# One VectorE subtraction of 1024 columns written as two of 512, in a fused gate-and-FFN kernel on one Trainium2 core

## The reference

```python
ctx   = causal_ema(x, tau_ctx)                        # h[t] = alpha*h[t-1] + x[t]
gated = x * sigmoid(concat([x, ctx]) @ Wg.T + bg)
h1    = gelu(x @ Wn1.T + bn1)
mod   = 0.5 + sigmoid(h1 @ Wn2.T + bn2)               # (b, t, 128): one value for each trace d
traces_d = causal_ema(gated * mod[..., d], tau_d)     # 128 traces
temporal = sum_d traces_d * softmax(blend)[d]
out   = layernorm((gelu(x @ Wsoma.T + bsoma) * sigmoid(temporal @ Wtemp.T + btemp)) @ Wout.T)
scores, idx = top_k(out @ w_router, 16)               # of 32 time steps, for each batch
y     = x + out, and at idx also + sigmoid(scores) * (gelu(out[idx] @ W1 + b1) @ W2 + b2)
```

## Time and profile before

| what | value |
|---|---|
| time, median of 3 runs | 177.53 us (177.35 to 177.87) |
| the profiled execution's own time | 177.58 us |
| its span, first to last instruction | 175.9 us |
| PE busy | 164.4 us (93%) |
| DVE busy | 132.8 us (76%) |
| POOL busy | 128.2 us (73%) |
| ACT busy | 93.2 us (53%) |

### The profile page before, as it was taken

How to read it: one execution, slowest core, us unless ns; L and a number is a source line. 1 busy time by engine, 2 the same in 40 slices (tenths; PEclk the granted TensorE clock), 3 DMA queues, 4 the chain that set the end, 5 groups by cost and what they waited for, 6 DMA issues and landing times.

```text
span 175.9 us, 3161 instructions
## 1 busy us (share of the span) xinstructions
PE 164.4 (93%) x1076; PEld 123.8 (70%) x1076; DVE 132.8 (76%) x188; ACT 93.2 (53%) x160; POOL 128.2 (73%) x129
## 2 busy tenths in 40 slices
PE   6579899999999999999889999999999999899991
PEld 6343558597557775798564779787939869888881
DVE  1577698977985987987999798788866757868413
ACT  0682997676524724553353943535274479557420
POOL 7726804999335899689999998999889749199900
PEclk9978999999999999999999999999999999999999
DMA  3995000000000000000000000000000040040214
GB/s 98 248 254 152 0 4 0 0 2 6 0 0 0 4 0 0 0 4 0 0 0 0 4 0 2 0 4 0 0 6 0 0 121 0 4 119 0 83 40 119
DMA packets 12767, 5.60 MB, mean 32 GB/s; under 512 B 2864, under 2 KB 12624, under 8 KB 12752
## 3 DMA queue, kind: packets, MB, share of 16 engines
q1 hardware_dynamic: 11696, 5.20, 11.3%
q10 hardware_dynamic: 1056, 0.20, 0.7%
HBM read 3.30 MB, written 2.10 MB: 31 GB/s over the span
## 4 chain that ended last, share of the span: by engine, by line
PE 74%; DVE 10%; issue 5%; POOL 4%; ACT 2%; ACTq 2%; DVEq 0%; POOLq 0%
PE ring L1085 21%; PE ring L1158 6%; PE ring L1140 5%; PE ring L1041 5%; POOL ctx_acc L506 4%; PE ring L1057 4%; PE ring L1101 4%; PE ring L1042 4%; PE ring L1068 3%; PE ring L1020 3%; PE ring L1109 3%; PE ring L1168 3%; PE ring L1095 2%; PE ring L1145 2%; DVE mod_lo L814 2%
## 5 line engine op out<-in xcount | busy, mean ns | idle before, releaser
L506 POOL TENSOR_TENSOR ctx_acc<-ctx_acc,prod 128x640 f32<-128x640 f32 (+10 forms) x44 | 69.1, 1579 | 16.0 <-DVE prod L847 12.4
L847 DVE TENSOR_TENSOR prod<-ring,gm 128x640 f32<-128x640 f32 (+10 forms) x44 | 34.8, 818 | 7.2 <-PE ring L1085 6.1
L1085 PE MATMUL ring<-mod_hi,decayed_lo 128*128 128x512 f32 (+7 forms) x80 | 25.0, 377 | 0.9 <-DVE state L834 0.8
L1085 PE MATMUL ring<-mod_hi,decayed_hi 128*128 128x512 f32 (+7 forms) x80 | 22.5, 347 | 0.0
L1085 PE MATMUL ring<-mod_lo,decayed_hi 128*128 128x512 f32 (+7 forms) x80 | 22.5, 346 | 0.0
L834 DVE TENSOR_TENSOR state<-ring,blend_w 128x1024 f32<-128x1024 f32 x16 | 18.8, 1216 | 1.8 <-PE ring L1057 1.8
L1085 PEld LDWEIGHTS ring<-mod_hi,decayed_lo 128*128 128x128 f32 x80 | 13.9, 188 | 7.4 <-issue 5.1
L1085 PEld LDWEIGHTS ring<-mod_lo,decayed_hi 128*128 128x128 f32 x80 | 14.5, 188 | 1.2 <-issue 0.2
L1158 PE MATMUL ring<-w_sb,gm 128*128 128x128 f32 x128 | 15.2, 276 | 0.0
L1085 PEld LDWEIGHTS ring<-mod_hi,decayed_hi 128*128 128x128 f32 x80 | 14.5, 188 | 1.0
L1158 PEld LDWEIGHTS ring<-w_sb,gm 128*128 128x128 f32 x128 | 14.8, 192 | 0.3 <-ACT gm L710 0.2
(11 more groups left out here) (168 smaller groups left out, 357.4 us busy)
## 6 DMA issues: line engine op xcount, KB each, us to landing
x_nat<-in_x_dram SPq DMA_DIRECT2D x4, 512.0 KB, 5.4
out_dram<-x_nat SPq DMA_DIRECT2D x3, 512.0 KB, 3.2
w_sb<-in_L_ffn_W_dram SPq DMA_DIRECT2D x2, 256.0 KB, 4.2
out_dram<-x_nat SPq DMA_DIRECT2D x2, 256.0 KB, 2.4
down<-in_cond_dram SPq DMA_DIRECT2D x2, 64.0 KB, 4.7
prod<-in_L_cond_Wg_dram ACTq DMA_DIRECT2D x1, 128.0 KB, 4.4
prod<-in_L_cond_Wsoma_dram ACTq DMA_DIRECT2D x1, 64.0 KB, 4.5
bn<-in_L_cond_bn_dram ACTq DMA_DIRECT2D x4, 0.1 KB, 4.3
```

The costliest lines, as they stand in the source:

```text
L506: nc.gpsimd.tensor_tensor(dst, dst, packed(prod[:, n % NP, 0:width(r)], r, k), ALU.add).then_inc(acc_done, 1)
L847: nc.vector.tensor_tensor(dst, packed(slot(step), r, k), lagged(gated(r), r, k), ALU.mult).then_inc(read(step), 1)
L1085: last = nc.tensor.matmul(to[:, c], w[:, k, :], src[:, c], start=(i == 0), stop=(i == len(parts) - 1))
```

## The change

The subtraction of `low:r` is written as two instructions, on columns 0 to 511 and 512 to 1023 of the round. The first has the waits that the single one had; the second follows with no wait of its own and alone counts up `split_done`.

```diff
-                    nc.vector.scalar_tensor_tensor(
-                        out=mod_lo[:, r % 2, 0:width(r)], in0=tmod(r), scalar=2.0,
-                        in1=mod_hi[:, r % 2, 0:width(r)].bitcast(F32), op0=ALU.add,
-                        op1=ALU.subtract).then_inc(split_done, 1)
+                    for half in (slice(0, BANK), slice(BANK, width(r))):
+                        last = nc.vector.scalar_tensor_tensor(
+                            out=mod_lo[:, r % 2, half], in0=tmod(r)[:, half], scalar=2.0,
+                            in1=mod_hi[:, r % 2, half].bitcast(F32), op0=ALU.add, op1=ALU.subtract)
+                    last.then_inc(split_done, 1)
```

## The result

The changed kernel took 180.05 us, the median of four runs (179.15 to 181.86), against 177.7 us before. The ratio is 1.012, 95% interval 1.009 to 1.0149, or 2.1 us more (1.6 to 2.65); it leaves out the longest of the four, which counts as a slow run. Forecast were 179.6 us and a slower kernel.

What follows compares the result with a forecast made beforehand. TensorE, busy 93% of the span, bounds the kernel, losing time where it waits. Terms 0.84 (`low:1`), 0.06 (`low:2`) and 1.14 (`low:3`) sum to 2.04; 177.53 + 2.04 gives 179.6 us, range 177.5 to 180.2.

Steps and rivals of the forecast that it cites:

- What the subtraction waits for: VectorE's subtraction reads nothing until GpSimd's running instruction ends; a half ends 0.54 us after it, GpSimd's add 1.14 to 1.16 after a subtraction.
- Who goes first at the seam: Between the two halves a waiting GpSimd instruction goes first, costing 1.14 us each at `low:1` and `low:3`; both seams, chance 0.50.
- the mirror image: Near 85.54 us before the change: waiting VectorE got in between two GpSimd instructions that followed each other without a gap.
- the forecast's last rival: At `low:2` VectorE starts before GpSimd's add: 0.2 us saved less 0.06, 177.4; chance 0.30 shared with VectorE keeping its turn.
- The rival that VectorE keeps its turn: Between halves VectorE goes on and GpSimd waits: 0.06 us twice, 177.7, no measurable change; chance 0.30 shared with `low:2` winning its race.
- The plain cost: The second instruction by itself: +0.06 us for a pair held behind GpSimd, +0.07 for a free pair (1.28 for 1.21).
- `low:3`: Near 86 us GpSimd's sum goes between the halves; second half ends at 87.76 instead of 86.62, +1.14 us on the chain.
- `low:1`: Near 34 us GpSimd's add goes between the halves: +1.14 us, less 0.36 cover, so TensorE waits +0.84 at `nat:0.1`.
- What GpSimd has of it: At `low:3` GpSimd gets its sum 0.54 us sooner, which no row shows anybody waiting for.

Runs made afterwards that it cites:

- the repeat: The changed kernel run once more with no edit: 179.91 us against 177.62 for the kernel before, ratio 1.0135.
- the single splits: Two runs of the changed kernel with only one subtraction left in halves: only `low:1`, 178.63 us, ratio 1.0057; only `low:3`, 178.67 us, ratio 1.0055.
- the quarters: The changed kernel with only `low:3` split, into four instructions of 256 columns, the other subtractions single: 182.86 us, ratio 1.0244.

## Why the prediction was right

**What the subtraction waits for.** Right, and to a few hundredths: behind a GpSimd instruction a half ends 0.54 to 0.56 later in every case, a GpSimd add of 512 columns 1.12 to 1.15 behind a half.

**Who goes first at the seam.** This was the one step without a row, taken from the mirror image in the earlier trace rows. Every seam with GpSimd waiting went that way: both in the first profile, both in the repeat, the one in each of the single splits, all three with the quarters. It isn't a strict taking of turns, though. At `low:2` GpSimd went twice running: its add, recorded from 71.13, went in behind its own `plus_beta:1`, ahead of VectorE's subtraction, recorded from 71.16; in the changed kernel it was 74.18 against 74.19, so VectorE lost again the race that the forecast's last rival had it win. What fits everywhere is that the instruction with the earlier recorded start goes first. The nine profiles that are read here have 38 hand-overs of these additions and subtractions, and of the tables' instructions on lines 472 and 783, at which the next instruction of both engines was already recorded as started. In all 38 the earlier one went first, four times between two VectorE instructions of line 783, which the change doesn't touch. This is read off recorded starts, some only 0.01 to 0.05 apart; no run set their order on purpose.

That this is what costs, holding GpSimd back showed: 1.0009 with all eight instructions in place. The rival that VectorE keeps its turn is out.
**The plain cost.** 0.06 was forecast at `low:2`; the pair ended 0.07 later behind GpSimd, and the chain shows +0.12 and +0.07. A free pair takes 1.28 for 1.21: its second half is recorded 0.68 long, but starts about 0.08 before the first ends. The estimate of 0.16 from the Trainium skill ("VectorE: DVE Perf Modes", section on the TRN2 errata) leaves that overlap out, and is too high here. At `low:0` the forecast put the 0.07 at nothing, as covered. In the first profile it was not: TensorE had waited for 2.25 us and began its first unit 0.25 behind the pair's end (25.06 against 24.81), as it did behind the single instruction with `plus_beta:2` moved (24.78 against 24.53). It is too little to show in the times.

**`low:3`.** 1.14 forecast; +1.15 and +1.13 in the two profiles, 1.0 alone (0.6 to 1.3).

**`low:1`.** Right in its mechanism, but the 0.84 was too small: +0.97 and +1.41 in the profiles, 1.0 alone (0.6 to 1.4). Two parts were left out. On the chain the four transposes that had to wait took 0.65 to 0.66 in place of 0.44, in both profiles: before, the first of them, recorded from 36.25, had overlapped the product in front, and behind a wait there is nothing to overlap. And the phase of GpSimd's adds against `low:1`, which I took from one execution, differs between executions (the one in front ends at 33.90 before, 34.20 in the repeat), so that TensorE's wait was 0.72, 1.20 and 0.76 in three profiles.

**What GpSimd has of it.** I said that its sum would be 0.54 sooner and nobody would wait for it. It was, but the second half then held the next add (2.74), and one instruction later all but 0.07 of the gain was gone.

The sum of 2.04 compares with 2.1 (1.6 to 2.65) and, in the repeat, 2.4 (1.9 to 2.9): it lies in both intervals, on the low side, for want of the 0.1 to 0.6 at `low:1`.

## What to carry to other kernels

Where VectorE and GpSimd exclude each other, as two instructions with both sources in SBUF do here, an instruction's length is also a hold on the other engine: splitting one on the critical path buys a turn for whoever is waiting, and the price is that engine's instruction, not the start of one's own. Before splitting, look in the timeline for what the other engine has ready at the seam; where that is nothing, a split is nearly free. The better lever is to have nothing of the other engine in front: moving two GpSimd adds that nobody needed for over 70 us gave 1.4%.

## What the runs showed of the hardware that was not expected

With the quarters TensorE waited 3.58 us, until 90.84. In the products behind that wait, at 92.0, its granted clock fell to 0.50; then it waited another 0.74 for the state read. Behind no other profiled wait near 90 us did the clock fall (0.71 and 1.02 us in the repeat). One stretch each: length, busy us of PE, PEld, DVE, ACT, POOL, granted clock, DMA share, GB/s:

```profile
90.80:92.00 1.20, 1.16 (x5) 1.01 (x6) 1.20 (x2) 0.00 (x0) 0.82 (x1) 1.00 0.00 0
92.00:94.00 2.00, 1.26 (x5) 0.53 (x4) 2.00 (x3) 0.00 (x0) 0.00 (x0) 0.50 0.00 0
94.00:96.00 2.00, 2.00 (x9) 2.00 (x9) 1.07 (x2) 0.00 (x0) 0.00 (x0) 0.50 0.00 0
96.00:98.00 2.00, 2.00 (x8) 2.00 (x7) 0.90 (x2) 0.00 (x0) 1.59 (x2) 0.50 0.00 0
...
98.60:100.00 1.40, 1.40 (x18) 1.18 (x21) 0.90 (x2) 0.46 (x2) 1.32 (x3) 0.92 0.00 0
```

At 0.50, the lower of its two levels, 1.2 GHz, the 18 products of units 2.6, 3.4 and 2.5 took 5.56 us where 3.18 stood, 2.4 more:

```profile
93.50 5.56 PE ring L1086 x18
```

That execution took 183.97 us, with a mean granted clock of 0.977. The clock at one half from 92.0 to 98.8 us takes 0.019 off such a mean (6.8 x 0.5 / 182.3). The other two runs of over 183 us, 183.09 and 184.59, had means of 0.972 and 0.977. The three of 181.72, 181.73 and 182.63 had 0.994, 0.988 and 0.989, too high for a fall of that length. So it seems that three of the six runs lost the clock there and three did not; the middle one of those three is 4.2 us above the kernel before, where the seams were expected to cost 4.0.

The first profile of the change has a fall too, behind a wait of 2.25 us for the first unit (0.50 from 26.3 to 29.6 us). In the profile with `plus_beta:2` moved TensorE waited 1.82 us at the same place, and its clock stayed at 1.00.
